# A hand-written row of turns for the drain of a woven recurrence and attention, and five distances moved beside it

## What is computed

```python
def _L0_attn_ref(x, ...):                  # the recurrence and its network
    h = _ln(x, ln1_g, ln1_b)
    real, imag = split(einsum('bsd,fd->bsf', h, W_to))
    def step(carry, u):                    # 1024 steps, one after the other
        sr, si = carry; r, i = u
        sr = sr * decay + r * 0.1
        si = si * decay + i * 0.1
        nr = clip(sr * c - si * s, -10.0, 10.0)
        ni = clip(sr * s + si * c, -10.0, 10.0)
        return ((nr, ni), (nr, ni))
    x2 = x + einsum('bsf,df->bsd', spectral_out, W_from) * 0.1
    h = _ln(x2, ln3_g, ln3_b)
    h = gelu(einsum('bsd,ed->bse', h, W_ffn1) + b_ffn1)
    return x2 + (einsum('bse,de->bsd', h, W_ffn2) + b_ffn2) * 0.1

def _L0_xattn_ref(query, key, value, ...): # 16 heads of 16
    attn = softmax(Q @ K.T / sqrt(16))
    return (attn @ V) @ Wo.T + bo

x = layernorm(x + _L0_attn_ref(x, ...))
x = layernorm(x + _L0_xattn_ref(x, ctx, ctx, ...))
x = layernorm(x + _L0_ffn_ref(x, ...))     # ternary weights, 8 bit rows, convolution
...                                        # the second layer
```

## Time and profile before

| | us |
|---|---|
| median of 3 runs | 2096.93 |
| lowest, highest | 2096.63, 2102.3 |
| the profiled execution | 2100.49 |
| its span, first to last instruction | 2098.4 |
| PE busy | 1762.4 (84%) |
| DVE busy | 1451.4 (69%) |
| ACT busy | 1041.7 (50%) |
| POOL busy | 491.6 (23%) |

### The profile page before, as it was taken

How to read it: one execution, slowest core, us unless ns; L and a number is a source line. 1 busy time by engine, 2 the same in 40 slices (tenths; PEclk the granted TensorE clock), 3 DMA queues, 4 the chain that set the end, 5 groups by cost and what they waited for, 6 DMA issues and landing times.

```text
span 2098.4 us, 34752 instructions
## 1 busy us (share of the span) xinstructions
PE 1762.4 (84%) x12793; PEld 1268.4 (60%) x12793; DVE 1451.4 (69%) x4876; ACT 1041.7 (50%) x2594; POOL 491.6 (23%) x555
## 2 busy tenths in 40 slices
PE   3667777887878878999999999999879999989708
PEld 1345656665653455666667766666658998974307
DVE  6887888887325886777776577777546667653795
ACT  5534555455437544555554455555125455433852
POOL 4101111011100223333333333333203332320002
PEclk8768988888969988999999999999999999999859
DMA  5000000000000101000000000000414433400001
GB/s 159 1 1 1 1 1 1 1 1 1 1 1 0 40 21 66 1 1 1 2 1 1 1 2 1 1 1 1 133 31 92 92 71 83 92 1 0 0 0 41
DMA packets 86363, 49.83 MB, mean 24 GB/s; under 512 B 40253, under 2 KB 83953, under 8 KB 86001
## 3 DMA queue, kind: packets, MB, share of 16 engines
q1 hardware_dynamic: 80337, 47.31, 8.7%
q10 hardware_dynamic: 5856, 0.29, 0.2%
HBM read 45.50 MB, written 2.10 MB: 23 GB/s over the span
## 4 chain that ended last, share of the span: by engine, by line
PE 55%; DVE 30%; ACT 8%; issue 4%; POOL 2%; DMA 1%; ACTq 0%; DVEq 0%; POOLq 0%
DVE sq L741 8%; DVE nx L738 8%; PE PS L1675 7%; PE PS L1702 6%; PE PS L1976 6%; PE PS L1689 5%; PE PS L1660 3%; PE PS L1647 3%; PE PS L2389 3%; PE PS L2039 2%; PE PS L1717 2%; PE PS L1995 2%; DVE nnm L1119 2%; PE PS L2004 2%; PE PS L1636 2%
## 5 line engine op out<-in xcount | busy, mean ns | idle before, releaser
L1832 POOL TENSOR_SCALAR px<-px,crl 128x128 f32<-128x128 f32 (+7 forms) x128 | 226.2, 1767 | 413.2 <-DVE crl L1804 413.2
L1741 ACT ACTIVATE px<-PS,cnm 128x128 f32<-128x128 f32 (+7 forms) x256 | 189.3, 740 | 261.6 <-DVE cnm L1789 254.7
L741 DVE TENSOR_SCALAR sq<-nx 128x4 f32<-128x4 f32 x1024 | 187.9, 184 | 35.0
L738 DVE TENSOR_TENSOR_SCAN nx<-sq 128x6 f32<-128x6 f32 x1024 | 182.9, 179 | 35.1 <-POOL sq L868 0.9
L1786 DVE TENSOR_REDUCE cm<-PS 128x1 f32<-128x128 f32 (+6 forms) x224 | 154.1, 688 | 56.7 <-PE PS L1675 56.1
L1689 PE MATMUL PS<-ident,px 128*128 128x128 f32 x1152 | 158.0, 278 | 14.1 <-ACT qT L1729 9.5
L1689 PEld LDWEIGHTS PS<-ident,px 128*128 128x128 f32 x1152 | 129.2, 141 | 61.6 <-issue 34.5
L1675 PE MATMUL PS<-kT,qT 64*128 64x512 f32 (+3 forms) x768 | 159.8, 521 | 5.0 <-ACT px L1741 2.6
L1702 PEld LDWEIGHTS PS<-pT,V 128*64 128x64 f32 x2304 | 124.1, 137 | 63.5 <-issue 34.5
L196 POOL TENSOR_SCALAR rstd<-mv 128x1 f32<-128x1 f32 x80 | 34.2, 427 | 540.0 <-DVE mv L174 540.0
L1702 PE MATMUL PS<-pT,V 128*64 128x128 f32 x2304 | 154.1, 278 | 5.9 <-DVE pT L1797 2.3
(11 more groups left out here) (335 smaller groups left out, 3935.3 us busy)
## 6 DMA issues: line engine op xcount, KB each, us to landing
xbs<-in_fside_Bx16xSxS SPq DMA_DIRECT2D x8, 1232.0 KB, 6.7
fsrc<-in_fside_Bx16xSxS SPq DMA_DIRECT2D x8, 1232.0 KB, 6.7
xmk<-in_mask_Bx16xSxS_bk SPq DMA_DIRECT2D x8, 308.0 KB, 8.5
fsrc<-in_mask_Bx16xSxS_bk SPq DMA_DIRECT2D x8, 308.0 KB, 8.4
X<-in_x SPq DMA_DIRECT2D x4, 512.0 KB, 6.7
w<-in_L_attn_W_ffn SPq DMA_DIRECT2D x2, 1024.0 KB, 12.7
t<-in_L_ffn_w SPq DMA_DIRECT2D x2, 1024.0 KB, 11.8
out<-xs SPq DMA_DIRECT2D x16, 128.0 KB, 1.7
```

The source lines that it names most:

```text
L738: e.tensor_tensor_scan(k.nx[:, :], d0, d1, 0.0, ALU.mult, ALU.add).then_inc(sem("rec.scan"), 1)
L741: e.tensor_scalar(o, bass.AP(k.nx, 2, [[6, P], [0, 2], [3, 2]]), 10.0, -10.0, ALU.min, ALU.max).then_inc(sem("rec.clip"), 1)
L1741: e.activation(k.px[n % 2][:, h, 0:width], src, ACT.Exp, scale=-1.0, bias=k.cnm[:, n % 4, h:h + 1], accum_out=k.cl[:, n % 4, h:h + 1]).the ...
L1832: e.tensor_scalar(k.px[n % 2][:, 0, 0:width], k.px[n % 2][:, 0, 0:width], k.crl[:, n % 4, 0:1], None, ALU.mult).then_inc(sem("c.normal0"), 1)
```

## The change

The distances of some steps in `network_chain` and `near_scores` change, and the rounds of the drain give way to a written string in which each letter is one turn of one chain: n for net, s for scores, u for sums, e for ends, t for begin.

```diff
+LAST = ("nusunuennsuesunsunusnuenuununnnuunsteststsutsutsuusueuuuuue")
@@ recurrence_order
-        while net.step:
+        while net.step and c < BT:
             net.offer(100)
-            if c == BT:
-                scores.offer(100)
-                sums.offer(100)
-                ends.offer(100)
     needs["taps", 0] = [("put", 2, NT - 1)]
-    begin = Chain(o, needs, ternary_begin())
-    while ends.step or begin.step:
-        scores.offer(100)
-        sums.offer(100)
-        ends.offer(100)
-        begin.offer(100)
+    chains = {"n": net, "s": scores, "u": sums, "e": ends, "t": Chain(o, needs, ternary_begin())}
+    for name in LAST:
+        chains[name].offer(100)
@@ network_chain
-    yield from norm(1, 2, 11, 4 if late else 13)
+    yield from norm(1, 3, 11, 0 if late else 13)
...
-    yield from norm(2, 12 if late else 20, 7, 5 if late else 10)
+    yield from norm(2, 12 if late else 20, 8, 5 if late else 10)
@@ near_scores
     yield 5, ("n.score", T, 0)
-    yield 24, ("n.top", T, 0)
+    yield 23, ("n.top", T, 0)
```

## The result

| | before | after |
|---|---|---|
| median | 2099.61 us (2096.63 to 2104.57, 4 runs) | 2085.51 us (2084.88 to 2086.79, 4 runs) |
| the profiled execution, its span | 2100.49, 2098.4 | 2086.79, 2084.7 |
| last recurrence step ends | 532.95 | 530.52 |
| first product row behind the drain | 634.92 | 619.41 |

The changed kernel takes 0.9931 of the time, 95% interval 0.9915 to 0.9947: 14.1 us less, where the prediction had 8.3 less (0.9960). The sign holds, and the time lies in the range, nearer to rival A (2084) than to the forecast (2088.6). That it lies in the range is partly luck: the prediction counted from 2096.93 us, and the kernel before had 2099.61 in this comparison. As a difference the range was 1.9 to 13.4 us less, and 14.1 is beyond it.

A forecast was written before the change was run, and what follows sets the result against it. DVE's scan and clip were taken to bound the recurrence, a chain hopping between PE, ACT and DVE the drain. Terms +0.4 - 1.6 - 0.9 - 2.9 - 2.2 - 1.1 = -8.3 us took 2096.93 to 2088.6 us; range 2083.5 to 2095.

The forecast's parts named there:

- rival A: Drain: less idle time of PE also gives back half-clock time, another 4.5 us, to 2084 us; chance 0.12.
- Chunk 2: Recurrence, chunk 2: work woven in one step later lengthens DVE's waits by one step in all, +0.4 us.
- Chunk 7: Recurrence, chunk 7: the turn of t = 6 ahead of the peak shortens DVE's 6.13 us wait, -1.6 us.
- Head of the drain: Drain's start: n.out of tile 13 fills PE's idle time before the first up of t = 7, -0.9 us.
- Norm of t = 7 to the maxima of tile 7: Drain: tile 14's norm and the next part's scales run earlier, so tile 7's maxima come sooner, -2.9 us.
- The rounds and turns: Drain, next part's chain: rounds no longer hold tile 15's first maximum, turns precede its second score, -2.2 us.
- The last tiles: Drain's end: n.back of tile 7 moves ahead of the peak, beside the maximum, -1.1 us.
- Rival B: Gain given back: a half-speed stretch shifts into the product behind the drain, +5 us, to 2094; chance 0.25.
- Rival C: Slower: in chunk 7 ups waiting for ACT lengthen DVE's wait, 2106 us at 2 us each; chance 0.05.

The follow-up runs named there:

- e3_turn_late: The changed kernel with the first norm's turn in chunk 7 put back four steps behind its scale; 0.9933 of the time of the kernel before.
- e4_begin_old: The changed kernel with the turns of the next part's chain (t) put back where the old round had them; 0.9955 of the kernel before.
- e7_busy_after: The changed kernel with 11 matmuls nobody reads added in six idle times of PE in the drain; 2079.05 us, 0.9894 of the kernel before.
- e5_head_old: The changed kernel with the old round up to n.back of tile 14, the new row from there; 0.9929 of the kernel before.
- fillers: Unread matmuls added in PE's idle times in the drain: 19 in the kernel before (2095.69 us, 0.9977), 11 in the changed kernel (2079.05 us, 0.9894).
- e10_all_adds_on_pe: The changed kernel with GpSimd's three additions to X beside the recurrence made matmuls against the identity on PE; 2070.26 us, 0.9851 of the kernel before.

## Why the prediction was right, and where not

**Chunk 2 (+0.4).** +0.1 by the waits of the profiled runs (4.36 to 4.45). The chunks 3 to 6 show no wait, as forecast. Right in sign, of no weight.

**Chunk 7 (-1.6).** The mechanism was right: the turn ran ahead of the peak, and the wait fell by 2.2 us (e3_turn_late brings it back). The size is partly luck. Peak and turned scores took 3.3 us instead of 5.9, at full clock, for which there was no term; the ups began 4.3 us sooner instead of 1.9, and the longer wait for the first gelu (1.53, not 0.8) and the gelus behind it took half of that back. ACT's table load was 1.28 us and the gelu followed at once (486.02, 487.32), as the prediction read from the trace before. The step that failed is the sentence that each us of DVE's wait is a us of the span. In the profiled run the 2 us were gone at the query of tile 14, since PE then idled for DVE and slowed down; in e4_begin_old and e7_busy_after they were kept.

**Head of the drain (-0.9).** -0.7 in this pair of traces (16.3 to 15.5 us from the recurrence's end to that query), with PE at half clock in it. Between the kernels where the rows right behind the recurrence ran at full clock it is -2.4 to -2.9. So the term is right in sign and too small, and the time of e5_head_old is too coarse to show it.

**Norm of t = 7 to the maxima of tile 7 (-2.9).** From the scores of tile 7 to the end of its second maximum it took 7.9 us before and 5.4 after: -2.5, for the reason given. Beside it stand two gains that I had no term for: -1.8 as the query of tile 7 ran at full clock, and -0.6 between the `down` and that query, where `unit` on DVE took 0.41 us instead of 0.81, without one of GpSimd's additions beside it.

**The rounds and turns (-2.2).** -4.8 in the traces, 5 by e4_begin_old. The step that failed is in the working: the 3.0 us of the turns were taken from rows of before, which were at half clock, as if a row's duration stayed when the idle time ahead of it goes, and the score's 1.1 stands in none of the rows shown. Turns took 2.0 us with their wait, and the score 0.65. With the clock kept up by fillers in both orders the stretch is 1.5 us shorter, less than forecast; the rest is clock.

**The last tiles (-1.1).** -2.1 to the mix and 0.7 more to the first product row. The `n.back` stands ahead of the peak (604.12), as forecast. What of the surplus is clock and what order wasn't taken apart.

**Rival A** was no rival but an addition. It had 4.5 us for the clock; the parts above without a term of their own, or over it (1.8, 2.6, 1.7), make 6.1, of which at least the 1.8 are clock by the row, and e4_begin_old shows the next. The fillers put the clock's part of the drain's gain at about 3.9. It stood at 0.12 because I held "the order decides" and "the clock decides" to be two cases, though the order is what takes the idle time away. The fillers settle that the clock is a cause: they move nothing and bring 9 us in the drain of before. The Trainium skill, "TensorE: Matmul & The Clock Gate", section "What's actually happening", was cited for A: activity releases the throttled state. The fillers agree, with 0.95 granted instead of 0.80.

**Rival B** took a small part. The product behind the drain kept its length (7.6 us from its first row to the next wait in both), but between about 1460 and 1550 us 2.0 us went back. The windows of that stretch, of before and after, 15 us apart as the work is:

```profile
1475.00:1495.00 20.00, 16.04 (x93) 13.27 (x90) 15.87 (x23) 2.96 (x7) 7.02 (x8) 1.00 0.88 302
```

```profile
1460.00:1480.00 20.00, 16.04 (x94) 13.06 (x90) 13.96 (x22) 2.96 (x7) 5.16 (x7) 0.91 0.85 293
```

The same 16.04 us of PE, but a granted clock of 0.91 against 1.00. Why the clock fell there, 800 us behind the change, no run shows. **Rival C** didn't come: the ups of chunk 7 waited 1.53 us once.

**GpSimd** is the cost that no case had. In the profiled pair it made 1.4 us of the difference by a coincidence of places, which e7_busy_after, with the same code there, doesn't show. I had read the recurrence's pace from one undisturbed step and taken it for all 1024.

What stays open: how the 14.1 us split between order and clock to better than 2 or 3 us, as in a chain of dependent rows each changes the other, and single profiled runs differ by as much. The recurrence ended between 528.4 and 531.0 us in five kernels with the new distances and the same code up to there, and between 532.9 and 536.1 in three with the old ones, so the gain there, 2.4 us in the first pair, is 4.8 between the means of the two groups.

## What to carry to other kernels

Where TensorE works in a chain with idle times, read a row's duration together with the idle time ahead of it, and cost a reordering twice, at both speeds of the row; the gain of filling an idle time includes the rows behind it. A place that is right where an engine idles is wrong where it would have to wait: move it in that chunk alone. Before ordering work around a serial chain on VectorE, compare the durations of the same small instruction all along it: the slow ones name the neighbour that costs.

## What the runs showed of the hardware

- Eleven matmuls whose results nobody reads made the changed kernel 6.5 us faster by the medians (2085.51 to 2079.05), 8 by the ratios; the same 16 matmuls take 1.95 to 2.05 us or 3.6 to 3.8.
- A scan of six columns and a clip of four take 0.65 us instead of 0.17 while GpSimd adds two tiles of 256 columns in SBUF; a maximum over PSUM (2.28 us) does not slow down, though GpSimd adds through all of it (472.76 in the changed kernel). The Trainium skill, "GPSIMD Engine Reference", section "1. Specifications", says that GpSimd's SBUF interfaces are shared with VectorE, with contention for instructions of two SBUF inputs or in a 2-port mode. The scan has two inputs, so its row agrees; the clip has one and was slowed as much, and whether it ran in such a mode no run here shows.
- Those additions, 0.7 us each on GpSimd, cost the recurrence 13 us of 530, and no row of the recurrence waited for their results. As a matmul against the identity, in a group that runs anyway, one of them over 256 columns took 0.59 us of TensorE, 0.43 from its start to the next row; DVE's waits in the recurrence grew from 8.4 to 11.8 us in e10_all_adds_on_pe, and its end still came 13 us sooner.
